# Flags by matmul, transposes at the beginning, loop hints on TensorE alone, last attention in a new order

## Chip, cores and metric

One core of a Trainium2 chip runs the whole program in one launch. The time is device microseconds of that core, as the median of several executions. One of them was also profiled; the profile's span runs from the first to the last instruction.

## The reference

The inputs are x (32 batches, 224 rows, 512), a context (32, 750, 384), a mask of rows, two gates and four weight matrices.

```python
def xattn(x, y, mask):                      # 16 heads of 32
    q = (x @ Wq.T), k, v = split(y @ Wkv.T)
    a = where(mask[:, None, :, None], q * 32**-0.5 @ k.T, -1e9)   # a masked row: all scores equal
    return softmax(a) @ v
def bitlinear(x, w, b):                     # rmsnorm, 8-bit rows, ternary weights
    return act_quant(rmsnorm(x)) @ weight_quant(w).T + b
x = x + tanh(g_xattn) * xattn(layernorm(x), ctx, mask)
x = x + tanh(g_ffn) * bitlinear(gelu(bitlinear(layernorm(x), w1, b1)), w2, b2)
```

weight_quant divides by the mean of |w| over the whole matrix, so no weight can be rounded before all have been read. A row outside the mask has equal scores, and its attention is the mean of v. With these inputs only the last quarter (56 rows) of a batch has rows that attend; the other three quarters use the mean.

## The kernel before, in words

All five engines have an instruction stream of their own, written out by hand, and meet by semaphores. The work has three parts.

**Beginning.** SyncE loads the context of batch 0 and the weights. ScalarE rounds them to the high part of a split of fp32 in two (`y_h`, `wkv_h`), VectorE takes the rest (`y_l`, `wkv_l`). VectorE reduces the mask bytes to `live_b` (a row for each batch), which SyncE brings through a DMA into one row, `live`; from that come `kind` (a number per batch) and `most` (their largest). Each engine's `Slow` loads `most` into a register, and `each` skips the code for batches that attend in more than the last quarter. There are none here, so all engines branch past it. GpSimd first increments some fifty semaphores by one (`primed`), and then fills the constants, the identity (`ident`) among them. TensorE waits for all six constants (`a_const`).

**Attention.** A period handles one batch b. It computes scores, softmax and weighted sum of b (four groups of four heads) interleaved with the k and v projections of batch b + 1, the loads of batch b + 2, and layer norm and quantising (the first half of the FFN) of batch b - 1: `summed` and `centred` and `rounded` on GpSimd, `x1_moments` and `x1_peak` on VectorE. One buffer set, f_x and f_c and so on, serves all batches; x1 and the rounded rows go to DRAM. Even and odd batches have different orders. In `batches`, every engine runs a period for batch -1 (projections alone), a loop of pairs up to batch 15, `middle`, a loop of pairs from batch 16 to 29, batch 30 written out, and `final` for batch 31. The loops carry a hint (`hint_back_edge`) for the branch at their end. Batches 0 to 15 also read a piece of w1 or w2 each, of which VectorE sums the magnitudes; in `middle` these sums become the mean (a matmul with `ones`), its inverse and three factors. Batches 16 to 31 read the pieces again, and GpSimd rounds them (`weights`).

**Last attention and FFN.** `final` interleaves batch 31's attention with the first steps of the FFN loop. There the 7168 rows go in 56 steps of 128: `inputs` (transpose), `widened` (first layer, 16 matmuls in two halves; VectorE adds b1 and scales), gelu and squares (ScalarE), root (GpSimd), `columns` (VectorE, its result is t_hs), `integers` (ScalarE), transposes, second layer, and the sum with x1 (GpSimd). TensorE works at transposes of step s - 2 and the second layer of step s - 3. The steps run as eight written out, a loop of eight (no hint), and the rest. The b1 row is loaded in `final`'s time and multiplied by a factor from the mean. Batch 31's layer norm is done in steps 2 to 7, in the same buffer set.

## Time and profile before

| | us |
|---|---|
| median of 3 executions | 1868.21 (1868.11 to 1868.63) |
| the profiled execution, its own time | 1867.66 |
| its span | 1865.9 |
| TensorE busy in the span | 1808.0 |
| VectorE, ScalarE, GpSimd busy | 1154.2, 990.6, 793.4 |

Times in the rows below are microseconds from the span's start. A row of the timeline has start, busy time, engine, line and operation, what it writes from what, shapes and count, and in brackets how long the engine was idle before and what released it. `issue` means that the profile shows nothing that it waited for.

### The profile page before, as it was taken

The numbers are of one execution on the slowest core, as the hardware profiler recorded it, in microseconds if no ns is written. First come the engines' busy times: TensorE is split into PE (matmuls) and PEld (weight loads), VectorE is DVE, ScalarE is ACT, GpSimd is POOL, SyncE is SP. The second block draws the span as 40 slices with busy tenths as digits, with TensorE's granted clock in tenths as the row PEclk, the third lists the DMA queues.
The fourth block names the chain that finished last, engine by engine and source line by source line (L and its number), as shares of the span: only waits on it lengthen the run. The fifth ranks groups of instructions, "written<-read, shape, count | busy, mean of one in ns | idle before, by whom it ended". The sixth has DMA issues, their size and how long they took to land.

```text
span 1865.9 us, 46309 instructions
## 1 busy us (share of the span) xinstructions
PE 1808.0 (97%) x16994; PEld 1395.2 (75%) x16995; DVE 1154.2 (62%) x2015; ACT 990.6 (53%) x1639; POOL 793.4 (43%) x1091
## 2 busy tenths in 40 slices
PE   5999999999999998999999999999977999999998
PEld 4888888888888887888888888888854555555554
DVE  2555556555555555555555555555558888888885
ACT  3444444444444443444444444444447888888886
POOL 1134344544433443556565555666544322222222
PEclk9999999999999999999999999999988999999999
DMA  4023322223223322222232232222133222222221
GB/s 146 14 79 108 91 88 73 78 73 93 73 80 113 90 81 74 79 73 78 74 92 73 82 119 85 78 73 73 61 103 100 78 85 84 76 79 84 82 91 44
DMA packets 83529, 153.91 MB, mean 82 GB/s; under 512 B 9725, under 2 KB 24061, under 8 KB 83341
## 3 DMA queue, kind: packets, MB, share of 16 engines
q1 hardware_dynamic: 83140, 152.89, 27.0%
q8 instruction: 33, 0.54, 0.1%
q10 hardware_dynamic: 328, 0.25, 0.1%
q14 instruction: 28, 0.22, 0.0%
HBM read 112.64 MB, written 40.46 MB: 82 GB/s over the span
## 4 chain that ended last, share of the span: by engine, by line
PE 89%; issue 3%; DVE 3%; ACT 2%; DMA 1%; POOL 1%; SPq 0%; POOLq 0%; DVEq 0%; ACTq 0%
PE psum L1383 23%; PE psum L1393 22%; PE psum L1403 9%; PE psum L1372 8%; PE psum L1618 8%; PE psum L1660 8%; PE psum L1412 5%; PE psum L1363 3%; PE psum L1646 2%; ACT hq L895 2%; DVE hid L1213 1%; PE psum L1420 1%; PE psum L1424 1%; DMA live<-live_b 1%; PE psum L1629 0%
## 5 line engine op out<-in xcount | busy, mean ns | idle before, releaser
L774 ACT ACTIVATE prob<-psum,nmax 114x750 f32<-114x750 f32 x256 | 225.5, 885 | 276.0 <-DVE nmax L1014 276.0
L1019 DVE TENSOR_TENSOR k_l<-psum,k_h 128x376 fp32r<-128x376 f32 (+1 forms) x256 | 139.7, 546 | 290.6 <-ACT k_h L765 290.6
L1383 PE MATMUL psum<-y_h,wkv_h 128*128 128x376 f32 (+1 forms) x768 | 277.2, 361 | 1.1 <-DVE q_l L1007 1.1
L1014 DVE TENSOR_REDUCE nmax<-psum 114x1 f32<-114x750 f32 x256 | 228.3, 933 | 76.2 <-PE psum L1372 73.4
L765 ACT ACTIVATE k_h<-psum 128x376 fp32r<-128x376 f32 (+1 forms) x256 | 124.0, 484 | 281.3 <-PE psum L1383 280.8
L1383 PE MATMUL psum<-y_l,wkv_h 128*128 128x376 f32 (+1 forms) x768 | 256.0, 333 | 0.0
L1383 PE MATMUL psum<-y_h,wkv_l 128*128 128x376 f32 (+1 forms) x768 | 255.7, 333 | 0.0
L1393 PE MATMUL psum<-wkv_h,y_h 128*125 128x512 f32 x576 | 239.0, 415 | 0.3 <-DVE wkv_l L1071 0.3
L340 POOL TENSOR_TENSOR f_x<-f_c,f_x 112x512 f32<-112x512 f32 x64 | 76.4, 1195 | 358.8 <-DMA f_c<-vmean_rows 338.1
L1393 PE MATMUL psum<-wkv_l,y_h 128*125 128x512 f32 x576 | 228.8, 397 | 0.0
L1393 PE MATMUL psum<-wkv_h,y_l 128*125 128x512 f32 x576 | 227.7, 395 | 0.0
L1618 PE MATMUL psum<-w_q,xq_t 128*128 128x512 bf16 x896 | 207.3, 385 | 4.1 <-DVE xq_t L1235 4.1
L1660 PE MATMUL psum<-w_q,hq_t 128*128 128x512 bf16 x896 | 202.6, 379 | 2.2 <-ACT yo L912 2.2
L1403 PEld LDWEIGHTS psum<-ident,prob 114*125 114x125 f32 x1536 | 186.0, 189 | 12.5 <-ACT prob L774 3.9
L1403 PE MATMUL psum<-ident,prob 114*125 114x114 f32 x1536 | 188.9, 273 | 5.5 <-ACT prob L774 5.5
L1028 DVE COPY prob_t<-psum 125x342 f32<-125x342 f32 x256 | 127.7, 510 | 96.5 <-PE psum L1403 85.7
L1618 PEld LDWEIGHTS psum<-w_q,xq_t 128*128 128x128 bf16 x896 | 84.6, 99 | 120.5 <-issue 21.5
L879 ACT ACTIVATE hid<-hid,gelu_in 128x1024 f32<-128x1024 f32 x112 | 127.8, 1143 | 82.3 <-DVE hid L1213 82.3
L607 POOL TENSOR_TENSOR y_l<-y,y_h 128x750 fp32r<-128x750 f32 x93 | 151.3, 1658 | 33.6 <-ACT y_h L760 33.6
L1660 PEld LDWEIGHTS psum<-w_q,hq_t 128*128 128x128 bf16 x896 | 85.2, 98 | 95.4 <-ACT yo L912 2.8
L1383 PEld LDWEIGHTS psum<-y_h,wkv_h 128*128 128x128 f32 x768 | 144.6, 188 | 14.7 <-DVE q_l L1007 1.5
L684 POOL TENSOR_SCALAR cols<-cols 128x1 f32<-128x1 f32 x56 | 10.8, 192 | 328.5 <-ACT hq L895 328.3
(120 smaller groups left out, 3372.2 us busy)
## 6 DMA issues: line engine op xcount, KB each, us to landing
y<-in_ctx_t SPq DMA_DIRECT2D x32, 1125.0 KB, 5.8
w_part<-in_w_t SPq DMA_DIRECT2D x32, 512.0 KB, 7.1
x_rows<-f_x SPq DMA_DIRECT2D x64, 224.4 KB, 2.8
x<-x_rows SPq DMA_DIRECT2D x56, 256.5 KB, 2.8
f_x<-in_x SPq DMA_DIRECT2D x64, 224.0 KB, 5.4
out_rows<-yo SPq DMA_DIRECT2D x56, 256.0 KB, 2.0
f_c<-vmean_rows SPq DMA_DIRECT2D x32, 224.0 KB, 6.2
xq_rows<-f_q SPq DMA_DIRECT2D x64, 112.0 KB, 2.7
```

The source lines that it names most:

```text
L607: pool.tensor_tensor(y_l[:, slot, c, :], y[:, c, :], y_h[:, slot, c, :].bitcast(F32), ALU.subtract).then_inc(f.yl, 1)
L774: act.activation(prob[:, e, :], ps_score[e][0:RP], ACT.Exp, bias=nmax[:, i:i + 1], accum_out=den[:, i:i + 1]).then_inc(p.exp, 1)
L879: act.activation(seg, seg, ACT.Gelu, scale=gelu_in[:, 0:1]).then_inc(t_g, 1)
L1014: dve.tensor_reduce(nmax[:, i:i + 1], ps_score[e][0:RP], AX.X, ALU.max, negate=True).then_inc(p.max, 1)
L1019: dve.tensor_tensor(k_l[:, g, s0:s1], ps_proj[k_bank[par][g, hf]][:, 0:s1 - s0], k_h[:, g, s0:s1].bitcast(F32), ALU.subtract).then_inc(f.k ...
L1028: dve.tensor_copy(prob_t[:, g % 2, e, MH:MJ, :].rearrange("p j n -> p (j n)"), ps_pt[e][1]).then_inc(p.pd, 1)
L1372: mm = pe.matmul(ps_score[e][0:RP, s0:s1], qs[r, slot, g, :, :].rearrange("p e r -> p (e r)"), ks[r, g, s0:s1], start=(n == 0), stop=(n == 2))
L1383: mm = pe.matmul(out_, ws[:, c, w], ys[:, slot, c, s0:s1], start=(c == 0 and n == 0), stop=(c == CC - 1 and n == 2))
L1393: mm = pe.matmul(out_, ys[:, slot, c, mcols], ws[:, c, D:], start=(c == 0 and n == 0), stop=(c == CC - 1 and n == 2))
L1403: mm = pe.transpose(ps_pt[e][hf][:, RP * j:RP * j + RP], prob[:, e, MC * jj:MC * jj + MC], ident[0:RP, 0:RP])
L1618: mm = pe.matmul(out_[:, BANK * o:BANK * o + BANK], xq_t[:, j % 2, 128 * c:128 * c + 128], w1_q[:, c, at_:at_ + BANK], start=(c == 0), sto ...
L1660: mm = pe.matmul(ps_y, hq_t[:, (j - LAG) % 2, 128 * c:128 * c + 128], w2_q[:, c, :], start=(c == 0), stop=(c == FC - 1))
```

## The change

- Flags: `live_rest` and `kind` are computed with a batch per partition in fp32 (`kind_b`), and turned into a row by a matmul with the identity into PSUM, which VectorE copies. The DMA goes. `ident` is filled before the `primed` increments, whose order changes. VectorE's and TensorE's `Slow` move ahead of other work.
- Beginning: TensorE issues 20 transposes of the identity, after three parts of y_h.
- Hints: only TensorE's two attention loops carry the hint; TensorE's batches 16 and 17 are written out (`peeled`).
- Mean: TensorE's matmul of `middle` moves behind the first scores of batch 16.
- Last attention: another order on VectorE and on TensorE, VectorE takes the two copies of the last group from ScalarE, GpSimd's `weights` goes first. SyncE issues the w2 piece ahead of the FFN's loads. Batch 30's layer norm is split between `final` and steps 2 to 7, batch 31's uses a second buffer set in v's slot 0 and goes on to step 48.

```diff
+        end_ = v[0:PT, 0].rearrange("p j n -> p (j n)")
...
+        sets.append((two(cut(2 * (D + 1))), two(cut(2 * D)), two(cut(D).bitcast(BF16)), two(cut(12)), two(cut(4)), two(cut(16))))
...
-        ENDS = (NT * 128 - S) // 128
+        ENDS = [(B - 2 + i) * S // 128 for i in range(2)]
...
-        primed = (a_w, a_wuse, a_wsum, a_wmm, a_wmean, c_st, *main.primed(), *aside.primed(), *last.primed(), *rest.primed())
+        primed = (*main.primed(), *last.primed(), a_w, a_wuse, a_wsum, a_wmm, a_wmean, c_st, *aside.primed(), *rest.primed())
...
-        def loop(eng, start, end):
-            return nc.Fori(start, end, engines=[eng.engine], hint_back_edge=True)
+        def loop(eng, start, end, hint):
+            return nc.Fori(start, end, engines=[eng.engine], hint_back_edge=hint)
...
-            with loop(eng, B // 4, B // 2 - 1) as t:
+            for b in range(B // 2, B // 2 + 2 * peeled):
+                period(b, b % 2, B // 4, True)
+            with loop(eng, B // 4 + peeled, B // 2 - 1, hint) as t:
...
     SyncE
-                sp.wait_ge(a_flag, 1)
-                sp.dma_start(live[:], live_b[:]).then_inc(a_live, 16)
...
+                    if w == 1:
+                        sp.wait_ge(f.x1, 2 * q)
...
                     if is_step(s, 2):
-                        ffn_load(B - 1, B - 1, False)
-                        copy_one(B - 2, c_end[0])
+                        stored(B - 1)
+                        ffn_load(B - 1, B - 1, False, main, 1)
                     if is_step(s, NT - RING):
-                        ffn_store(B - 1, B - 1)
+                        ffn_store(B - 2, B - 2)
+                    if is_step(s, ENDS[0] - 2):
+                        ffn_store(B - 1, B - 1, main, x1_d, xq_d, 1)
...
+                w2_piece(B - 1, B // 8 - 1, 1)
                 step(-1, -1, 0)
+                step(0, 0, 0)
+                step(1, 1, 0)
                 stored(B - 2)
                 ffn_load(B - 2, B - 2, False)
-                w2_piece(B - 1, B // 8 - 1, 1)
-                step(0, 0, 0)
-                ffn_store(B - 2, B - 2)
                 results(B - 1)
-                stored(B - 1)
-                run_steps(sp, step, 1, NT + LAG + 2)
+                run_steps(sp, step, 2, NT + LAG + 2)
...
     GpSimd
+                pool.memset(ident[:], 0.0).then_inc(own_ident, 1)
+                pool.wait_ge(own_ident, 1)
+                pool.affine_select(out=ident[:], in_=ident[:], compare_op=ALU.not_equal, fill=1.0, base=0,
+                                   pattern=[[-1, 128]], channel_multiplier=1).then_inc(a_const, 1)
+                pool.wait_ge(a_const, 1)
                 for s in primed:
                     pool.sem_inc(s, ONE)
...
                     for h in range(2):
-                        if is_step(s, 3):
-                            summed(B - 1, h)
-                        if is_step(s, 5):
-                            centred(B - 1, h)
+                        if is_step(s, 4):
+                            summed(B - 1, h, main, 1)
+                        if is_step(s, 6):
+                            centred(B - 1, h, main, 1)
+                        if is_step(s, NT - RING):
+                            rounded(B - 1, h, main, 1)
+                    for h in range(2):
+                        if is_step(s, 4):
+                            centred(B - 2, h)
                         if is_step(s, 7):
-                            rounded(B - 1, h)
+                            rounded(B - 2, h)
 
                 def final():
-                    for part in (summed, centred, rounded):
-                        for h in range(2):
-                            part(B - 2, h)
+                    weights(B - 1)
+                    for h in range(2):
+                        summed(B - 2, h)
                     step(1, 1, 0)
-                    weights(B - 1)
...
     ScalarE, final
-                    for e in range(2):
-                        first_half(last, n1, NG - 1, e)
...
     VectorE
-                dve.wait_ge(a_live, 16)
-                dve.tensor_reduce(live_rest[:], live[:, :, 0:NBLK - 1], AX.X, ALU.max).then_inc(a_flag, 1)
+                dve.wait_ge(a_flag, 1)
+                dve.tensor_reduce(live_rest[:], live_b[:, 0:NBLK - 1], AX.X, ALU.max).then_inc(a_flag, 1)
...
+                dve.wait_ge(a_live, 1)
+                dve.tensor_copy(kind[:], ps_kind).then_inc(a_flag, 1)
...
                     for h in range(2):
-                        if is_step(s, 4):
-                            x1_moments(B - 1, h)
+                        if is_step(s, 2 + h):
+                            x1_moments(B - 2, h)
+                        if is_step(s, 5):
+                            x1_moments(B - 1, h, main, 1)
                         if is_step(s, 6):
-                            x1_peak(B - 1, h)
+                            x1_peak(B - 2, h)
+                        if is_step(s, 7):
+                            x1_peak(B - 1, h, main, 1)
...
                     negated_max(last, n0, 0, 0)
                     negated_max(last, n0, 0, 1)
-                    dve.wait_ge(b_bias, 16)
-                    dve.tensor_scalar(b1_row[:], b1_row[:], bias_out[:], 1.0, ALU.mult, ALU.mult).then_inc(b_b1, 1)
                     second_half(last, n1, 0, 0)
                     second_half(last, n1, 0, 1)
                     inputs(0, 0)
                     negated_max(last, n0, 1, 0)
                     negated_max(last, n0, 1, 1)
+                    dve.wait_ge(b_bias, 16)
+                    dve.tensor_scalar(b1_row[:], b1_row[:], bias_out[:], 1.0, ALU.mult, ALU.mult).then_inc(b_b1, 1)
                     heads_out(last, b, 0)
-                    x1_moments(b - 1, 0)
-                    dve.wait_ge(b_b1, 1)
-                    widened(0, 0, 0, 0)
                     second_half(last, n1, 1, 0)
                     second_half(last, n1, 1, 1)
                     inputs(1, 1)
-                    x1_moments(b - 1, 1)
+                    dve.wait_ge(b_b1, 1)
+                    widened(0, 0, 0, 0)
...
+                    for e in range(2):
+                        second_half(last, n1, 3, e)
+                        dve.wait_ge(last.pt, n1 + (2 * (2 * 3 + e) + 1))
+                        dve.tensor_copy(prob_t[:, 1, e, 0:MH, :].rearrange("p j n -> p (j n)"), ps_pt[e][0]).then_inc(last.pa, 1)
                     widened(1, 1, 0, 0)
-                    second_half(last, n1, 3, 0)
-                    second_half(last, n1, 3, 1)
                     inputs(2, 2)
+                    heads_out(last, b, 3)
+                    peak(0, 0)
                     widened(1, 1, 0, 1)
-                    heads_out(last, b, 3)
                     divided(last, b, 32 * b + ONE)
-                    peak(0, 0)
...
     TensorE
-                pe.wait_ge(a_const, 6)
+                pe.wait_ge(a_const, 1)
+                pe.wait_ge(a_flag, 3)
+                pe.matmul(ps_kind, kind_b[:], ident[0:B, 0:B], start=True, stop=True).then_inc(a_live, 1)
+                pe.wait_ge(a_const, 7)
+                slow_pe = Slow(pe, "pe")
...
                     scores(last, 0, 0)
+                    if means:
+                        pe.wait_ge(a_wsum, 1 + ONE)
+                        pe.matmul(ps_w, ones[:], w_sum[:], start=True, stop=True).then_inc(a_wmm, 1)
...
+                    if means:
+                        pe.wait_ge(a_wmean, 1 + ONE)
                     weighted(last, n0, 0, 0)
...
                     inputs(2, 2, 0)
-                    widened(1, 1, 1)
                     pe.wait_ge(t_xe, 3)
                     weighted(last, n0, 1, 3)
+                    widened(1, 1, 1)
...
-                batches(pe, period, middle, final)
+                pe.wait_ge(a_yh, CC + ONE)
+                for i in range(20):
+                    pe.transpose(ps_warm, ident[:], ident[:])
+                batches(pe, period, lambda: None, final, 0, True, 1)
```

## Rows read from the trace of the kernel before

**Rows 1.** The page: span, chain that ended last by engine, a costly group.

```profile
span 1865.9 us, 46309 instructions
...
PE 89%; issue 3%; DVE 3%; ACT 2%; DMA 1%; POOL 1%; SPq 0%; POOLq 0%; DVEq 0%; ACTq 0%
...
L684 POOL TENSOR_SCALAR cols<-cols 128x1 f32<-128x1 f32 x56 | 10.8, 192 | 328.5 <-ACT hq L895 328.3
```

**Rows 2.** Chain that ended last, in order of time, 0 to 80: start, us, what.

```profile
6.14 9.70 DMA live<-live_b
...
22.75 4.17 PE psum L1393 x9
26.92 2.11 PE psum L1383 x9
29.03 2.11 PE psum L1393 x9
```

**Rows 3.** Timeline of GpSimd, 0 to 32.

```profile
6.61 0.10 POOL L592 MEMSET half<- 128x1 f32 x1 [6.15 <-issue]
```

**Rows 4.** Timeline of ScalarE, 0 to 32.

```profile
15.00 1.91 ACT L741 ACTIVATE wq_s<-w_q 128x2048 f32<-128x2048 f32 x1 [1.55 <-DMA w_q<-in_wq_t]
...
22.48 0.55 ACT L748 ACTIVATE xn_t<-psum 128x456 f32<-128x456 f32 x1 [5.48 <-PE psum L1356]
```

**Rows 5.** Timeline of TensorE, 0 to 60.

```profile
21.45 0.99 PE L1356 MATMUL psum<-ident,xa 114*128 114x114 f32 x4 [21.45 <-DVE xa L1000]
```

**Rows 6.** Timeline of TensorE: first scores of batches 14 to 18.

```profile
640.85 0.48 PE L1372 MATMUL psum<-k_h,q_h 64*114 64x512 f32 x2
...
680.75 0.48 PE L1372 MATMUL psum<-k_h,q_h 64*114 64x512 f32 x2
...
727.08 0.48 PE L1372 MATMUL psum<-k_h,q_h 64*114 64x512 f32 x2 [0.85 <-DVE w_cols L1197]
...
773.93 0.48 PE L1372 MATMUL psum<-k_h,q_h 64*114 64x512 f32 x2
...
817.72 0.49 PE L1372 MATMUL psum<-k_h,q_h 64*114 64x512 f32 x2
```

**Rows 7.** Timeline of VectorE, 718 to 738.

```profile
725.64 0.15 DVE L1189 TENSOR_REDUCE w_sum<-w_sums 128x2 f32<-128x16 f32 x1
...
727.07 0.20 DVE L1202 TENSOR_SCALAR y_out<-w_mean,gates 128x1 f32<-128x1 f32 x1
733.72 0.69 DVE L990 BATCH_NORM_STATS2 x_stats<-xa 114x6 f32<-114x512 f32 x1 [6.45 <-issue]
```

**Rows 8.** DMA queues, 720 to 740: queue, packets, MB, share.

```profile
q14 instruction: 3, 0.02, 0.3%
```

**Rows 9.** Timeline of TensorE, 1350 to 1425.

```profile
1370.65 0.97 PE L1372 MATMUL psum<-k_h,q_h 64*114 64x512 f32 x4 [5.59 <-DVE prob_t L1028]
...
1372.80 3.59 PE L1618 MATMUL psum<-w_q,xq_t 128*128 128x512 bf16 x8
...
1380.53 0.60 PE L1372 MATMUL psum<-k_h,q_h 64*114 64x512 f32 x4 [1.57 <-DVE prob_t L1028]
...
1381.75 1.90 PE L1618 MATMUL psum<-w_q,xq_t 128*128 128x512 bf16 x8
...
1405.97 1.89 PE L1646 MATMUL psum<-ident_h,hq 128*128 128x128 f16 x16 [5.33 <-ACT hq L886]
...
1419.37 3.62 PE L1660 MATMUL psum<-w_q,hq_t 128*128 128x512 bf16 x16
```

**Rows 10.** Timeline of VectorE, 1350 to 1425.

```profile
1368.37 1.28 DVE L1272 TENSOR_SCALAR b_row<-b_row,bias_out 128x2048 f32<-128x2048 f32 x1 [5.54 <-DMA b_row<-in_b]
1369.58 0.93 DVE L1028 COPY prob_t<-psum 125x342 f32<-125x342 f32 x2
...
1386.62 1.27 DVE L364 TENSOR_REDUCE f_cols<-f_c 112x1 f32<-112x512 f32 x2
...
1403.32 0.21 DVE L1227 TENSOR_SCALAR cols<-cols,y_out 128x1 f32<-128x1 f32 x1 [2.26 <-issue]
```

More of the change, by code:

```diff
@@ L271, in each, with batches @@
                     self.eng.sem_inc(met_slow, 1)
-        def loop(eng, start, end):
-            return nc.Fori(start, end, engines=[eng.engine], hint_back_edge=True)
-        def batches(eng, period, middle, final, first=0):
+        def loop(eng, start, end, hint):
+            return nc.Fori(start, end, engines=[eng.engine], hint_back_edge=hint)
+        def batches(eng, period, middle, final, first=0, hint=False, peeled=0):
             period(-1, 1, -1, False)
@@ L279, in batches @@
                 period(b, b, 0, False)
-            with loop(eng, first, B // 4) as t:
+            with loop(eng, first, B // 4, hint) as t:
                 for j in range(2):
@@ L1426, in sums, with even @@
                     mm.then_inc(p.rows, 1)
[L1428 removed]
+                def even(b, means):
                     n0, m = b * NP + ONE, b + 1
@@ L1593, in period @@
                     if j == 0:
-                        even(b)
+                        even(b, isinstance(b, int) and b == B // 2)
                     else:
                         odd(b, t, has_part(b), projects_ahead(b))
-                def middle():
-                    pe.wait_ge(a_wsum, 1 + ONE)
-                    pe.matmul(ps_w, ones[:], w_sum[:], start=True, stop=True).then_inc(a_wmm, 1)
-                    pe.wait_ge(a_wmean, 1 + ONE)
                 def low_halves(t, n):
```

90 lines of the change are left out of this document (49 added, 41 removed).

## The prediction

> **What bounds the kernel now.** The page comes first: span 1865.9 us, and the chain that ended last is TensorE for 89% [rows 1]. So what can be won is idle time of TensorE, and time in which it works at its lower clock (1.2 GHz and not 2.4). The second view to read is the start of each batch's first scores [rows 6]. From batch to batch they lie 39.90 us (even) and 43.79 us (odd) apart, without idle time inside. One pair stands out: 46.33 and 46.85 us where 43.79 and 39.90 are due, so the middle costs 2.54 + 6.95 = 9.5 us. The other two losses are at the ends of the attention: TensorE's first steady projection starts at 26.92 [rows 2], and between the last batch and the first second-layer matmul (1419.37 [rows 9]) stand idle times of 5.59 and 5.33 us [rows 9] and matmuls at half speed. The change touches all three places; I sum them against the profiled execution's own 1867.66 us, 1.8 us more than its span and 0.5 us under the median of 1868.21.
>
> **Start.** Before, VectorE sends the mask flags through a DMA; queued behind the big loads it lands 9.70 us later [rows 2], and everything VectorE does after it is late. The change replaces it by one small matmul on the identity, so GpSimd builds the identity before its 6.15 us of semaphore increments [rows 3] and not after them. VectorE's chain then follows its loads and is some 9 us earlier. What is late next? ScalarE, in whose order `turned` stands behind the wq copy: that waits for its load and runs 15.00 to 16.91 [rows 4]. Before, ScalarE turned only at 22.48; now it can from about 17.1, after the small `gates` and its branch past the unused code. The copy takes 0.55 us [rows 4], so the first k projection can start at 17.8, not 26.92: 9.1 us at best. Two things lie in between. The branch can need a code fetch; the two nearest prices are VectorE idles with no release in the profile, 2.26 us [rows 10] and 6.45 us under load [rows 7]. TensorE also issues 20 new transposes: four took 0.99 us at the low clock [rows 5], so 20 take at most 5.0 us; from the third y_h copy (about 9) they end at 14 if TensorE's own branch is through, at 17 if that is 3 us late, and then the 2.11 to 4.17 us of the first v chunk [rows 2] stand ahead of the k projection. I take a start at 19.2, nearer to the clean case since the copy hides most of the branch: 7.7 us. The lower bound is a k projection at 22.5 (fetch of 6.45 us from 16): 4.4 us. The transposes also raise the clock before the real work: nine v matmuls took 4.17 us and nine later ones 2.11 [rows 2]. The v part is now hidden in front of k; of k's 2.11 us, whose first half still ran at the low clock, I count 0.5 (0 to 1.0). Start: 8.2 us (4.4 to 9.6).
>
> **Middle.** The mean's tiny matmul now stands behind batch 16's first scores. That hides the 2.54 us wait: scores need nothing of the mean, and the sum is ready when they end. VectorE still runs its small instructions (from w_sum at 725.64 to y_out at 727.27, 1.6 us with their waits [rows 7]) ahead of the maxima of these scores, on which exp and the transposes wait. TensorE has two projections to do in between, so about 1.4 us of it shows. The other 6.95 us come from VectorE: it sat idle for 6.45 us with nothing that released it at its first instruction of the second loop [rows 7], TensorE then waited for exp and worked at the low clock around it. Three blocks of code were fetched in these 20 us [rows 8], while the same view over 200 to 460, loops running with hints, has none, nor has it over 1520 to 1760 (FFN loops, which carry no hint in either kernel). I read: the hint keeps the loop's head at hand and leaves the code behind the loop to be fetched after the exit. Without hints on VectorE the 6.95 go. Middle: 9.5 - 1.4 = 8.1 us (0 if the stall stays, 9.5 at most).
>
> A page speaks against this edit. The Trainium skill, Runtime: NRT & Kernel Launch, section Instruction fetch mechanics, says that prefetch is sequential and that a taken branch to a target outside the window of two pages has to be fetched first. By that an unhinted back edge could stall each time. The trace has the stall at the exit, not at the FFN loops' unhinted edges, so the rule's condition (a body too long for the window) decides; it is the fourth case below. TensorE keeps its hints and gets two batches outside the loop; they are the same instructions without the branch, and I cost that at nothing.
>
> **Last attention and ramp.** (a) VectorE idled 5.54 us for the b1 row [rows 10] ahead of the copies that free the score banks, and TensorE 5.59 us with it [rows 9]. Now two copies, `inputs` and two maxima (3 to 4 us of work) come first, by when the row has landed. The release for TensorE's second scores moves from behind the scaling's end (1369.65) and two copies to where VectorE's idle of 5.54 us began, less what the transposes take: near 1365.4 in place of 1370.65, 5.2 us. (b) They and the next eight matmuls ran at the low clock: 1370.65 to 1372.80 and 3.59 us, later 1380.53 to 1381.75 and 1.90 us [rows 9]. Without the pause: 0.9 + 1.7 = 2.6 us. (c) VectorE sheds two statistics with a small instruction each (the like of them took 0.69 us [rows 7]) and two peaks (1.27 together [rows 10]), some 2.9 us, and takes over two half copies from ScalarE, 0.9 us: 2.0 net; half of it is on the path, 1.0. (d) GpSimd's rounding of the w2 piece moves before the first FFN row's root, and TensorE's last weighted sum ahead of the last hidden matmul: 0.9 us, within the bound 0 to 2. (e) The 2.26 us idle without a releaser in `columns` [rows 10] is of the fetch kind and sets t_hs, ScalarE's integers and TensorE's 5.33 us idle. It goes with the hint or comes back elsewhere; I take 2.0. Against it: the w2 piece is now issued ahead of xq and x1 of step 1, so the second `inputs` waits about 0.6 us. Sum 5.2 + 2.6 + 1.0 + 0.9 + 2.0 - 0.6 = 11.1. The other ramp idles stay. Bounds: 7 (c to e nothing, b half) to 15 (all, and the 5.33 us idle short enough that the clock stays up).
>
> **What is moved into the FFN.** Batch 30's layer norm now runs in steps 2 to 7, batch 31's up to step 48, in a second buffer set lying in the v slot that the last attention doesn't read. GpSimd idles 328.5/56 = 5.9 us per step ahead of its root [rows 1]. Step 4 gets two sums and two centrings, about 8 us, so 2 us over: that delays one root by 2 us, against VectorE's and ScalarE's idle time before it. Cost 0, at worst 2 us once. VectorE gets at most 1.7 us more in a step. The loads and stores (SyncE) are issued some steps ahead of the rows that need them: nothing. The price if that cover is gone is one late store, 3 us.
>
> **Sum.** 8.2 + 8.1 + 11.1 = 27.4. 1867.7 - 27.4 = 1840.3; with the 0.5 us to the median, 1840.8 us.
>
> **Rivals.**
> 1. The forecast: 1841, own range 1834 to 1848. Chance 0.62.
> 2. The exit stall is no matter of hints: any first entry to new code costs VectorE a fetch, at 727 under a 1.1 MB load. For it: straight code in `columns` stalled too. Against: in the whole list of waits these two are VectorE's only idles without a releaser, and its first loop's first entry has none. The 6.95 us stay, and with the delayed mean the middle gives 1 us: 1848. Chance 0.17.
> 3. A new wait in the last attention: xq and x1 behind the w2 piece, or ScalarE's table load and gelu setting the pace, and low clock through the ramp as before. The end gives 5 us in place of 11.1: 1847. Chance 0.13.
> 4. The other side: unhinted back edges stall. VectorE's two attention loops have six back edges each, at the even batch's start, where the middle showed what an idle of 6.45 us costs TensorE: 6.95 us. 12 x 6.95 = 83 us, 1841 + 83 = 1924. For it: VectorE's attention body is longer than its FFN body of eight steps, and it is the only one with this length. Against: the FFN body is nearly as long and fetches nothing. It decides from 27.4/12 = 2.3 us per edge on, about the smaller of the two idle times. Chance 0.06.
> 5. Small cover losses at all places: 1855 to 1866. Chance 0.02.
>
> **Range and chances.** Cases 1 to 3 lie between 1834 and 1855; with case 4 and what lies beyond left out, 1834 to 1853 holds about 8 in 10. A difference of 0.2% (3.7 us) is about what a measurement can tell from none. Faster: cases 1, 2, 3 and most of 5, 0.92. Same 0.02, slower 0.06.
>
> **What would show it.** After: no DMA of `live`; first steady k projection near 19 us; first scores of batches 15 to 17 about 43.8 and 39.9 us apart, 1.4 more in all, with no idle of VectorE over 2 us; b1's scaling without idle ahead of it; second-layer matmuls of step 0 some 27 us earlier than 1419.37; FFN steps as long as before. Wrong if code fetches appear every 84 us on VectorE with idle behind them, if ScalarE's first turn comes later than 21, or if GpSimd's step 4 makes TensorE idle.

## The result and the profile after

The kernel after takes 1852.89 us (median, 1851.26 to 1853.91), the kernel before on the same chip 1868.36: ratio 0.9919 [0.9904, 0.9934]. The forecast was 1841, with 1834 to 1848 as its own range and 1834 to 1853 for about 8 in 10. The sign was right, but the gain was 15.5 us where 27.4 were forecast; that the time lies 0.1 us inside the wider range confirms nothing. The profiled execution after took 1853.91 us with a span of 1852.2, so 13.7 of span were gained against the 1865.9 of [rows 1].

Read the timeline of TensorE in the order of the chain. The first group is the beginning, beside [rows 2] and [rows 5]:

```profile
15.41 4.50 PE L1808 MATMUL psum<-ident 128*128 128x128 f32 x20 [10.12 <-issue]
19.70 0.97 PE L1390 MATMUL psum<-ident,xa 114*128 114x114 f32 x4
20.35 0.73 PE L1427 MATMUL psum<-wkv_h,y_h 128*125 128x512 f32 x1
...
22.76 0.34 PE L1417 MATMUL psum<-y_h,wkv_h 128*128 128x376 f32 x1
...
50.49 0.60 PE L1406 MATMUL psum<-k_h,q_h 64*114 64x512 f32 x4
```

TensorE stood idle until 15.41 with nothing in the profile that it waited for (`issue`), then ran the 20 transposes, and only then turned xa. ScalarE, which the prediction took for the limit, waited for it:

```profile
17.44 0.19 ACT L771 ACTIVATE gates<-gates_in 128x2 f32<-128x2 f32 x1
20.71 0.55 ACT L776 ACTIVATE xn_t<-psum 128x456 f32<-128x456 f32 x1 [3.08 <-PE psum L1390]
```

The first k projection starts at 22.76 (before 26.92, forecast 19.2), the first scores at 50.49, where they were at 55.05: 4.6 us. The middle, beside [rows 6] (first scores of batches 15 to 17):

```profile
676.21 0.60 PE L1406 MATMUL psum<-k_h,q_h 64*114 64x512 f32 x4
...
719.99 0.60 PE L1406 MATMUL psum<-k_h,q_h 64*114 64x512 f32 x4
...
725.90 0.91 PE L1437 MATMUL psum<-ident,prob 114*125 114x114 f32 x6 [0.48 <-ACT prob L802]
...
761.66 0.60 PE L1406 MATMUL psum<-k_h,q_h 64*114 64x512 f32 x4
```

The distances are 43.78 and 41.67 us, where they were 46.33 and 46.85. And VectorE's first instruction of the second loop comes without the 6.45 us of [rows 7]:

```profile
722.52 0.21 DVE L1231 TENSOR_SCALAR y_out<-w_mean,gates 128x1 f32<-128x1 f32 x1
722.96 0.69 DVE L1019 BATCH_NORM_STATS2 x_stats<-xa 114x6 f32<-114x512 f32 x1 [0.24 <-DVE y_out L1231]
```

All steady distances are as before (39.91 and 43.78 us), but one is new: batch 30, right behind the exit of TensorE's second loop, takes 43.36 us where 39.91 are due. TensorE stops inside its first scores with no releaser in the profile, and then works at the low clock for some 3 us (0.63 us for a matmul that takes 0.39):

```profile
1307.56 0.49 PE L1406 MATMUL psum<-k_h,q_h 64*114 64x512 f32 x2
1309.65 0.37 PE L1406 MATMUL psum<-k_h,q_h 64*114 64x238 f32 x2 [1.60 <-issue]
...
1311.26 0.63 PE L1427 MATMUL psum<-wkv_h,y_l 128*125 128x512 f32 x1
...
1314.25 0.48 PE L1417 MATMUL psum<-y_h,wkv_h 128*128 128x376 f32 x1
...
1350.92 0.60 PE L1406 MATMUL psum<-k_h,q_h 64*114 64x512 f32 x4
```

The last attention and the ramp, beside [rows 9]. From batch 31's first scores to the first second-layer matmul it is 1350.92 to 1401.52, 50.60 us, where it was 59.63:

```profile
1357.05 0.97 PE L1406 MATMUL psum<-k_h,q_h 64*114 64x512 f32 x4 [0.27 <-DVE prob_t L1057]
...
1359.11 1.90 PE L1652 MATMUL psum<-w_q,xq_t 128*128 128x512 bf16 x8
...
1378.32 0.81 PE L1446 MATMUL psum<-prob_t,v 125*32 125x57 f32 x48 [2.40 <-DVE xq_t L1264]
1379.06 3.29 PE L1652 MATMUL psum<-w_q,xq_t 128*128 128x512 bf16 x8
...
1387.67 1.07 PE L1680 MATMUL psum<-ident_h,hq 128*128 128x128 f16 x16 [1.10 <-ACT hq L914]
...
1394.10 6.47 PE L1652 MATMUL psum<-w_q,xq_t 128*128 128x512 bf16 x16 [5.14 <-DVE xq_t L1264]
```

The FFN, where the prediction had nothing to lose, loses 2.2 us: from the first to the eleventh second-layer matmul it is 82.51 us, before 80.29. The timeline of GpSimd in step 4 (from 1409.16 sums and centrings without a gap, then the root at 1417.33, with no idle time before it):

```profile
1409.16 2.34 POOL L356 TENSOR_TENSOR v<-v 112x512 f32<-112x512 f32 x2
...
1416.16 1.09 POOL L377 TENSOR_TENSOR f_x<-b_row,f_x 112x512 f32<-112x512 f32 x1
1417.33 0.19 POOL L708 TENSOR_SCALAR cols<-cols 128x1 f32<-128x1 f32 x1
```

VectorE's columns wait for that root, ScalarE's gelu waits for what VectorE adds behind them, and the distance of ScalarE's squares, about 8.1 to 8.3 us elsewhere, is 10.00 there:

```profile
1418.19 0.21 DVE L1252 TENSOR_SCALAR cols<-cols 128x1 f32<-128x1 f32 x1 [1.88 <-POOL cols L710]
```

```profile
1413.23 1.89 ACT L923 ACTIVATE hq<-hid 128x2048 bf16<-128x2048 f32 x1
...
1420.19 1.15 ACT L907 ACTIVATE hid<-hid,gelu_in 128x1024 f32<-128x1024 f32 x1 [2.70 <-DVE hid L1242]
...
1423.23 1.89 ACT L923 ACTIVATE hq<-hid 128x2048 bf16<-128x2048 f32 x1
```

At the very end one second-layer group takes 5.32 us; the same sixteen matmuls take 3.63 at the high clock, as they did in the profiled execution of before: 1.7 us.

```profile
1833.29 5.32 PE L1694 MATMUL psum<-w_q,hq_t 128*128 128x512 bf16 x16 [1.40 <-ACT yo L940]
1838.44 1.06 PE L1680 MATMUL psum<-ident_h,hq 128*128 128x128 f16 x16
1839.39 3.63 PE L1694 MATMUL psum<-w_q,hq_t 128*128 128x512 bf16 x16
```

| part | forecast | measured |
|---|---|---|
| start (first scores of batch 0) | 8.2 | 4.6 |
| middle (first scores 15 to 17) | 8.1 | 7.7 |
| batch 30 | 0 | -3.45 |
| last attention to first second layer | 11.1 | 9.0 |
| FFN ramp and loop | 0 | -2.2 - 0.2 |
| clock at the end | 0 | -1.7 |
| sum | 27.4 | 13.75 |

### The profile page after: what moved, and what is told of

Same layout as the page of the kernel before. It is cut to its first block, busy times and chain, and to the rows that moved or that the text cites. A ratio compares the mean times of both kernels' runs of the same rounds, so it can differ in the third digit from the quotient of the medians.

```text
span 1852.2 us, 46262 instructions
## 1 busy us (share of the span) xinstructions
PE 1811.3 (98%) x17016; PEld 1395.8 (75%) x17017; DVE 1153.6 (62%) x2018; ACT 989.3 (53%) x1637; POOL 791.9 (43%) x1091
## 4 chain that ended last, share of the span: by engine, by line
PE 89%; issue 4%; DVE 3%; ACT 3%; POOL 1%; DMA 0%; POOLq 0%; DVEq 0%; ACTq 0%
PE psum L1417 23%; PE psum L1427 22%; PE psum L1437 9%; PE psum L1406 8%; PE psum L1652 7%; PE psum L1694 7%; PE psum L1446 5%; PE psum L1397 3%; ACT hq L923 2%; PE psum L1680 2%; DVE hid L1242 1%; PE psum L1454 1%; PE psum L1458 1%; POOL cols L710 0%; PE psum L1390 0%
## 5 line engine op out<-in xcount | busy, mean ns | idle before, releaser
L708 POOL TENSOR_SCALAR cols<-cols 128x1 f32<-128x1 f32 x56 | 10.7, 190 | 331.1 <-ACT hq L923 331.0
```

## The experiments

Each of the sixteen kernels is the kernel after with the edit shown, if nothing else is said. A ratio is to the kernel before on the same chip, whose medians were 1865.79 to 1867.33 us there, against 1868.36 beside the kernel after. So a difference of under some 3 us between two medians tells nothing. For single microseconds the distances inside the traces are used, one profiled execution each; the start (first scores at 49.6 to 50.5 in nine executions with the same beginning) and the end (below) scatter in these too.

### The hints

Hints back on all engines (`hint=True` as the default in `batches`, so on the loops of VectorE, ScalarE and GpSimd together):

> The kernel after, with the hint on the attention loops of all engines again, as before the change. Theory A (the hint is what made VectorE idle for 6.45 us at its first instruction of the second loop): the idle time returns in the middle, at x_stats, and the distance of the first scores of batches 16 and 17 goes from 41.67 to about 48 us: 6 to 7 us more, 1859.5. Theory B (any first entry to new code costs it; in the kernel after it only fell well): the distance stays at 41.7 and the time at 1852.9. Steady distances (39.91 and 43.78 us) stay in both.

Measured: 1860.26 us, 0.9963 [0.9949, 0.9977]; batch 16 takes 49.39 us and not 41.67. VectorE's timeline has both idles without a releaser again, that of the middle and, 1.7 us of loss in the ramp (52.30 us for 50.60), that of `columns`:

```profile
728.38 0.69 DVE L1019 BATCH_NORM_STATS2 x_stats<-xa 114x6 f32<-114x512 f32 x1 [6.33 <-issue]
...
1399.05 0.21 DVE L1252 TENSOR_SCALAR cols<-cols 128x1 f32<-128x1 f32 x1 [2.79 <-issue]
```

The other direction, the kernel before with this one part of the change, again for these three engines together:

> The kernel before with one part of the change alone: the hint on TensorE's two loops only, none on the other engines' attention loops. Theory A (the hint on VectorE made its idle of 6.45 us at the second loop's first instruction): that idle goes, first scores of batches 16 and 17 stand 39.9 to 41.5 us apart and not 46.85, batches 15 and 16 still 46.3; the last attention also gains the 1.7 us that the reverse test lost: 1860 in all. Theory B (the gain in the middle came from where the mean's matmul stands and from the two batches written out, the hint only decides together with them): under 2 us of gain, 1866 or more.

Measured: 1857.63 us, 0.9958 [0.9944, 0.9972]. Batch 15 still 46.33, batch 16 now 41.40; x_stats starts 0.24 us after the instruction ahead of it:

```profile
726.92 0.69 DVE L990 BATCH_NORM_STATS2 x_stats<-xa 114x6 f32<-114x512 f32 x1 [0.24 <-DVE y_out L1202]
```

The last attention takes 55.19 us where it took 59.63: 4.4 us more gained, from the hints alone. In spans, this one edit gives 10.2 us, where the whole change gives 13.7. Theory A, larger than expected. That VectorE's hint is the one that counts among the three is read from its idle times and was not tried by itself.

No hint at all, TensorE's last argument pair `True, 1` made `False, 1`:

> The kernel after, without the hint on TensorE's two loops either, so that no loop of the kernel carries it. Theory A (for TensorE the hint keeps the pass running at the loop's end; without it the head of the loop is fetched after the branch): an idle of 1 to 4 us at each of TensorE's back edges, twelve or thirteen in all, first scores of even batches late by that: 1865 to 1900. Theory B (as on VectorE, a back edge without a hint costs nothing, and the exit gets better): distances of 43.78 and 39.91 us in all pairs, batch 30 too: 1849.5.

Measured: 1896.72 us, 1.0149 [1.0117, 1.0181]. Most batches of both loops take 1.4 to 2.8 us more, with 2.2 us idle at a back edge. The view of the DMA queues says why: q8, which brings TensorE's code in blocks of 16 KB, has no entry from 200 to 600 after, and here

```profile
q8 instruction: 42, 0.69, 0.7%
```

So an unhinted back edge does cost on TensorE (2.17 us of `issue` at 224.66, for one), while the kernel after has no idle time of that kind on VectorE.

### Where TensorE's code lies

The same edit in several sizes, in `slow_first`, which no engine executes here:

```diff
                     pe.wait_ge(a_wqs, 1)
+                    for _ in range(64):          # 192 and 128 in the next two
+                        pe.wait_ge(a_wqs, 1)
```

> The kernel after, with 64 more wait instructions for TensorE in the code for batches that attend in more than the last quarter. No engine executes that code with these inputs; it only moves all TensorE code behind it by 64 instructions. Theory A (the 43.36 us between the first scores of batches 30 and 31, where 39.91 is due, come from where TensorE's second loop ends against the blocks in which its code is fetched): the distance is 39.9 again, no idle of TensorE without a releaser stands behind the loop's exit, and the time is 3.4 us lower than the kernel after, near 1849.5. Theory B (leaving a hinted loop costs TensorE a fetch wherever its code lies, or the stall belongs to the two batches written out): the distance stays at 43.4 and the time at 1852.9. In both, the branch at the start may cost more or less than before, by up to 3 us, which is read from TensorE's first transposes.

Measured: 1882.96 us, 1.0084 [1.0067, 1.0101]. Batch 30 takes 39.91 us, as theory A has it, but batches 19 to 28 take up to 46.3 us, 28.8 more in all, and batch 16 takes 4.2 more. The DMA view of 900 to 1300 (none of these rows in the kernel after):

```profile
q8 instruction: 40, 0.66, 0.7%
```

40 blocks in 400 us are nine for each pass of some 89 us, while a pass has 1843 instructions in the trace, 7.2 blocks.

> The kernel after, with 192 more wait instructions for TensorE in the code that no engine executes, where the run before this one had 64. TensorE's code is fetched in blocks of 16 KB, 256 instructions of 64 bytes, so 192 more is the same place in the blocks as 64 fewer. One pass of an attention loop has some 1843 instructions on TensorE in the trace's records, 7.2 blocks. Theory A (a loop whose body touches eight blocks stays, one that touches nine is fetched anew in each pass, and code just behind a block's border at the exit is late): the second loop ends some 80 instructions ahead of a border, so neither occurs: batches 19 to 29 at 43.78 and 39.91 us, batch 30 at 39.91, and 3.4 us less than the kernel after, 1849.5. Theory B (every shift away from the code's old place has such a cost, by something other than blocks): losses in several batches as in the run with 64.

Measured: 1894.68 us, 1.0142 [1.0122, 1.0162]. Now the second loop and batch 30 are clean (43.78, 39.91), and the first loop is fetched anew: batches 1 to 14 take 43.3 to 46.4 us. The same view, 200 to 600:

```profile
q8 instruction: 41, 0.67, 0.7%
```

> The kernel after, with 128 more wait instructions for TensorE that no engine executes. Theory A (what decides is where a loop lies against the blocks of 256 instructions; the second loop lies 57 further in a block than the first, by the number of instructions in the trace; a shift of 64 costs the second loop, 192 the first, so the costly part reaches at least from 121 to 192 behind the first loop's old place): with 128 the first loop is at 128 and the second at 185, both inside, so both are fetched anew in each pass: batches 1 to 14 and 19 to 29 each 1 to 5 us longer, about 70 us in all, 1915 to 1930. Theory B (the place of each loop decides in no such simple way): only one loop or none is slower, under 1900.

Measured: 1851.60 us, 0.9921 [0.9904, 0.9937]. Neither loop is fetched anew, so theory A of this run fell. In its place the first loop's exit stalls (batch 15 at 45.88 us) and the second's doesn't (39.91):

```profile
721.82 0.60 PE L1406 MATMUL psum<-k_h,q_h 64*114 64x512 f32 x4 [2.03 <-issue]
```

I read: a loop of 7.2 blocks touches eight, or nine when its end lies a little behind a border. Eight stay, nine are fetched anew in each pass; an end just ahead of a border gives the stall at the exit. This picture is argued and not shown, since no trace has the addresses. For the second loop the stall is at shift 0 and the fetching at 64; for the first at 128 and at 192. That the two lie 128 apart, and not the 57 that I had counted, was fitted afterwards. And one thing it doesn't explain: with a shift by a whole block (three kernels below) batch 30 also takes 39.91 us. By the Trainium skill (Runtime: NRT & Kernel Launch, Instruction fetch mechanics) TensorE's instruction memory holds 2048 instructions and is filled in blocks of 256, which is eight blocks. The 0.66 MB in 40 packets agree with the block's size, and that nine blocks in a pass are fetched anew agrees with its eight. The window of two pages, which the prediction quotes from the same section of the Trainium skill, does not agree with TensorE's hinted loops here: passes of 7.2 blocks run from 200 to 600 with no entry on q8, and the measurement decides.

The stall at the exit is not the same in all kernels that have it. With the same TensorE code, the kernel of `The FFN's step` below (centring in step 3) idles a little less, its clock stays high, and batch 30 takes 41.60 us and not 43.36:

```profile
1309.45 0.37 PE L1406 MATMUL psum<-k_h,q_h 64*114 64x238 f32 x2 [1.43 <-issue]
```

So of the 3.45 us about half is the stall and half the low clock behind it.

### The start

Without the 20 transposes (their two lines deleted, 40 unexecuted instructions in their place):

> The kernel after, without the 20 transposes of the identity at the beginning; 40 instructions that no engine executes keep the code behind them in its place. Theory A (the transposes stand on the path, and the clock that they raise gives back less than they take): TensorE turns xa at 15.4 to 15.5, the first v chunk takes 4.0 to 4.2 us at the low clock, and the first scores of batch 0 start near 48.5 us where they start at 50.49 with the transposes; the time is 2 us lower. Theory B (the prediction's: they fit into waiting time and give a warm start): first scores at 50.5 or later, up to 51.2.

Measured: 1847.96 us, 0.9897 [0.9881, 0.9914]; first scores at 48.40. The transposes cost 2.1 us here; over all kernels, first scores stand at 49.6 to 50.5 in the nine with them behind the branch and at 47.1 to 48.4 in the five without any. The rest of this time's gain is not the start's: batch 30 takes 41.43 us, with an idle time of 1.45 and no low clock. Moved ahead of the branch instead:

```diff
+                for i in range(20):
+                    pe.transpose(ps_warm, ident[:], ident[:])
                 pe.wait_ge(a_const, 7)
                 slow_pe = Slow(pe, "pe")
```

> The kernel after, with the 20 transposes of the identity right behind the flags' matmul, ahead of the branch past the unused code and not behind it (and written to another bank). Theory A (the branch costs TensorE until about 15.4 whatever it does before, since a fetch stands behind it, and the transposes behind it then cost 4.5 us of the start): TensorE turns xa at about 15.5 where it did at 19.7, ScalarE's copy is ready at 17.4 to 18, the first k projection starts between 18 and 21 where it started at 22.93, and the time is 2 to 4 us lower, about 1850. The first v chunk may run at the low clock then, 4.2 in place of 2.25 us. Theory B (ScalarE, with the wq copy and the gates, is the limit of the start, or the fetch only begins when TensorE reaches the branch and is late by as much as the transposes take): the first k projection stays within 1 us of 22.9.

Measured: 1852.98 us, 0.9918 [0.9902, 0.9935], and yet first scores at 48.47; this profiled execution lost 1.2 us more than after at the end's clock. TensorE turns xa at 15.53, whether transposes were done before or not, and the clock has fallen again by then (0.63 us a matmul):

```profile
5.40 4.53 PE L1384 MATMUL psum<-ident 128*128 128x128 f32 x20
15.53 0.99 PE L1392 MATMUL psum<-ident,xa 114*128 114x114 f32 x4 [5.60 <-issue]
16.20 0.77 PE L1429 MATMUL psum<-wkv_h,y_h 128*125 128x512 f32 x1
16.77 0.63 PE L1429 MATMUL psum<-wkv_l,y_h 128*125 128x512 f32 x1
```

With 60 of them, to fill that idle time, and with the centring in step 3 (next section) and 176 unexecuted instructions:

> The kernel after with 60 transposes of the identity right behind the flags' matmul, ahead of the branch (another bank), in place of 20 behind it, and GpSimd's first centring of batch 30 in step 3; 176 instructions that no engine executes make the shift of TensorE's code a whole block. Theory A (TensorE's stream reads on while its matmuls run, so the fetch behind the branch overlaps the transposes, and they fill the idle time until 15.5 with work): the turn of xa still starts near 15.5, the first v chunk runs at the high clock (2.2 us and not 4.2), first scores at 46.5 to 47.5, time 1844 to 1845. Theory B (the fetch begins only when the transposes are through, near 14): the turn starts at 17 to 20 and the first scores stand at 48.5 to 50.5: 1847 to 1849.

Measured: 1850.25 us, 0.9907 [0.9893, 0.992]. Theory B: first scores at 50.26. The idle time moves with them, 4.09 us behind their end, and the clock is low all the same. The fetch moves too: the first block of TensorE's code behind the branch starts on q8 at 12.7 in the kernel after and in the two above, and at 14.7 here, and each time the first matmul follows its landing by 1.6 to 1.8 us.

```profile
4.88 8.79 PE L1384 MATMUL psum<-ident 128*128 128x128 f32 x60
17.77 0.99 PE L1392 MATMUL psum<-ident,xa 114*128 114x114 f32 x4 [4.09 <-issue]
```

### The FFN's step

GpSimd's first centring one step earlier:

```diff
                     for h in range(2):
-                        if is_step(s, 4):
+                        if is_step(s, 3 + h):
                             centred(B - 2, h)
```

> The kernel after, with GpSimd's first centring of batch 30 in FFN step 3 and not in step 4; the second stays. GpSimd's block in step 4 goes from 8.1 to some 5.4 us. Theory A (the FFN's step is set by a ring of squares, root, columns, second half of the first layer, gelu, squares, so that every delay of GpSimd's root is paid in full): root is not late in step 4, the distance of the squares there falls from 10.00 to about 8.6 us, and all later squares and the end come 1.4 us earlier, 1851.5. Theory B (the prediction's: TensorE has work to do meanwhile, and the delay is absorbed): the squares of steps 10 and later stand where they stood against the first squares, and the time is 1852.9.

Measured: 1849.47 us, 0.9905 [0.9889, 0.9922]. The squares of this stretch, 8.26 and 8.08 us apart:

```profile
1401.84 1.89 ACT L923 ACTIVATE hq<-hid 128x2048 bf16<-128x2048 f32 x1
1410.10 1.90 ACT L923 ACTIVATE hq<-hid 128x2048 bf16<-128x2048 f32 x1
1418.18 1.90 ACT L923 ACTIVATE hq<-hid 128x2048 bf16<-128x2048 f32 x1
```

First to eleventh second layer: 80.63 us for 82.51, 1.9 us kept to the end. This profiled execution is 6.4 us faster than that of the kernel after; the rest is batch 30 (1.8), the last attention (1.35) and the clock at the end (1.65), which the edit was not made for. The sharper test of what sets the step, one small instruction more in GpSimd's root:

```diff
+                        pool.tensor_scalar(c[:, HMS:HMS + 1], c[:, HMS:HMS + 1], 1.0, 0.0, ALU.mult, ALU.add).then_inc(own_ms, 1)
+                        pool.wait_ge(own_ms, 2)
                         pool.tensor_tensor(c[:, HR:HR + 1], c[:, HMS:HMS + 1], half[:], ALU.pow).then_inc(t_hr, 1)
```

> The kernel after, with one more small instruction of GpSimd (a multiplication by one) between the two of the FFN's root, in each of the 56 steps: some 0.28 us more in GpSimd's root, at an engine that idles for about 6 us in each step. Theory A (the ring of squares, root, columns, second half, gelu, squares sets the step of 8.14 us): the step becomes 8.4 us and the time 13 to 15 us more, about 1867. Theory B (the prediction's premise, TensorE sets the step and the other engines' idle time is cover): the step stays within 0.02 us of 8.14, and the time at 1852.9.

Measured: 1868.14 us, 1.0007 [0.9997, 1.0016]. 15.2 us more, from 0.27 us on an engine that is idle for some 6.1 in each step:

```profile
1602.32 0.19 POOL L708 TENSOR_SCALAR cols<-cols 128x1 f32<-128x1 f32 x1 [6.26 <-ACT hq L925]
1602.59 0.19 POOL L710 TENSOR_SCALAR cols<-cols 128x1 f32<-128x1 f32 x1
...
1610.73 0.19 POOL L708 TENSOR_SCALAR cols<-cols 128x1 f32<-128x1 f32 x1 [6.09 <-ACT hq L925]
```

The step is 1610.73 - 1602.32 = 8.41 us, where it was 8.14, and TensorE, without idle time there in the kernel after, now has some in each step:

```profile
1607.13 3.62 PE L1654 MATMUL psum<-w_q,xq_t 128*128 128x512 bf16 x16 [0.21 <-DVE xq_t L1266]
```

### The b1 row

VectorE's two lines with `bias_out` moved back ahead of `second_half(last, n1, 0, 0)`:

> The kernel after, with VectorE's scaling of the b1 row put back ahead of the copies of the first group, where it stood before the change. Theory A (the prediction's term: the wait for the row is worth 5.2 us, and the clock behind it up to 2.6 more): VectorE idles 3 to 6 us ahead of the scaling, TensorE's second scores start some 11 us after the first ones and not 6.1 us, and the first second-layer matmul stands 5 to 8 us later after batch 31's first scores: 1858 to 1861. Theory B (the row lands early enough now, or later waits, as ScalarE's, absorb the delay): under 2 us, 1853 to 1855.

Measured: 1858.80 us, 0.9956 [0.9939, 0.9972]. VectorE waits 5.36 us for the row again, and TensorE's second scores start 10.7 us after the first (in the kernel after, 6.1):

```profile
1361.31 0.97 PE L1406 MATMUL psum<-k_h,q_h 64*114 64x512 f32 x4 [4.51 <-DVE prob_t L1057]
```

But from batch 31's first scores to the first second layer it is 54.27 us for 50.60, so only 3.7 us reach the FFN. At the fourth group's weighted sum the difference is still 5.3 us: 1383.33 - 1350.59 = 32.74 here, 1378.32 - 1350.92 = 27.40 in the kernel after. The next eight matmuls and the last sixteen of the first layer are at the high clock for longer here, 1.90 us for 3.29 and 5.66 for 6.47:

```profile
1383.33 0.81 PE L1446 MATMUL psum<-prob_t,v 125*32 125x57 f32 x48 [2.40 <-DVE xq_t L1264]
1384.07 1.90 PE L1652 MATMUL psum<-w_q,xq_t 128*128 128x512 bf16 x8
...
1398.24 5.66 PE L1652 MATMUL psum<-w_q,xq_t 128*128 128x512 bf16 x16 [5.15 <-DVE xq_t L1264]
```

### The best version

Centring in step 3 and no transposes:

> The kernel after with two of the single changes together: without the 20 transposes (40 instructions that no engine executes in their place), and with GpSimd's first centring of batch 30 in FFN step 3. Theory A (the two gains are at different places of one chain and add): first scores near 48.4 us, 80.6 us from the first second-layer matmul to the eleventh, and 3.5 to 4.5 us less than the kernel after: 1846. Theory B (the second is taken back by VectorE's and ScalarE's own delays in steps 3 to 5): no more than 2 us less, 1848 or more.

Measured: 1844.24 us, 0.9875 [0.986, 0.989]. First scores at 47.06, first to eleventh second layer 80.58 us: both gains are there, the start's larger than by the single edit. Batch 30 takes 41.43. With 226 unexecuted instructions more:

> The run with both single changes together, with 226 more instructions that no engine executes, which is 30 fewer against the blocks of 256. Theory A (the stall behind the exit of TensorE's second loop goes when the code behind it lies a few instructions further from the border, and both loops still stay in the buffer): batch 30 at 39.91 us, all others as before, 1.5 to 3.5 us less than with both: 1843. Theory B (the first loop's head comes into the part of a block where the loop is fetched anew, as with 192): batches 1 to 14 each 2 to 5 us longer, 1890 or more.

Measured: 1889.85 us, 1.0112 [1.0092, 1.0133]: theory B, the first loop (40 blocks from 200 to 600). With a whole block more:

> The run with both single changes (no transposes, centring in step 3), with 256 more instructions that no engine executes. Theory A (the run with 60 transposes had batch 30 at 39.91 us because its code lay a whole block further, which pairs of blocks or the buffer's slots notice): batch 30 at 39.91 us, first scores of batch 0 near 47.1 to 48.4, 1.5 us less than without: 1842.7. Theory B (a whole block changes nothing; the clean exit there was another timing of the fetch): batch 30 at 41.4 us, 1844.2.

Measured: 1843.35 us, 0.9879 [0.9862, 0.9895], batch 30 at 39.91 in the profiled execution. The median is 0.9 us lower than without the block (the two kernels' executions overlap), so the gain itself is not shown. And with matmuls in the two idle times at the end (twelve of w1 against the identity in step 56, seven ahead of `pe.wait_ge(t_hq, k + 1)` behind a wait for t_he, five ahead of the wait for t_ye):

> The run with both single changes and the whole block's shift, with twelve extra matmuls of TensorE in FFN step 56, whose results nobody reads: seven ahead of the transposes that wait 1.75 us for ScalarE, five ahead of the second layer that waits 1.40 us. Theory A (these idle times let the clock fall in some executions, and the 16 matmuls behind them then take 6.55 us and not 3.63): the matmuls take 3.63 us, and the end stands 25.0 us after the fourth last second layer's start in all executions; times spread over less than 2 us, median 1 to 2 us below the same without them, about 1841. Theory B (the filling matmuls themselves delay the last steps, or the clock falls by another cause): the same time or up to 1 us more.

Measured: 1843.41 us, 0.9879 [0.9862, 0.9895], spread 1842.53 to 1844.10, against 1842.36 to 1844.87 without. The added matmuls cost nothing, and whether they hold the clock is not told: in both profiled executions the group behind them took 3.63 us. These last two are the best versions, 22.6 us under before on their chip, where the kernel after is 15.5 under before on its own.

## Where the prediction failed and where it held

Of the 13.65 us between the forecast's 27.4 and the table's 13.75, two terms that the prediction put at nothing make 5.9: batch 30 (3.45) and the FFN (2.4). Two that it mis-sized make 5.7: the start (3.6) and the last attention (2.1). The clock at the end (1.7), which it doesn't have, and the middle (0.4) are the rest.

**Start (8.2, measured 4.6).** The DMA wait and VectorE's delay went as said. The step that failed is the pricing of the 20 transposes and of the branch ahead of them: I let the transposes start at about 9, or 3 us later, and ScalarE's copy be the limit. TensorE, with the branch past the unused code in this stretch, stood idle until 15.41, 10.12 us after the flags' matmul; my worst case was 6.45 us of fetch from 16 on, a k projection at 22.5, and 22.76 lies just outside it. The transposes stood whole on the path behind it: 2.1 us net, since they spare 9 v matmuls the low clock but take 4.5. That the branch waits for a block of code is read from q8, whose block lands at 13.8 and moves with the transposes, and from the idle's `issue`; it was not isolated.

**Middle (8.1, measured 7.7).** The sum is right, and both reasons act. The wait of 2.54 us went, and 1.76 remained visible in batch 16 where 1.4 were forecast. But the shares are not the forecast's 6.95 for the hint and 1.1 for the mean, and that the sum fits is in part luck. Batches 15 and 16 together take 93.18 us before and 93.17 with all hints in the new order: as long as the hints are there, moving the mean and writing out two batches is worth nothing. Without the hints they are worth 2.3 (87.73 to 85.45), and the hints' going is worth 5.45 in the kernel before and 7.7 in the kernel after. Rival 2 is ruled out: the stall comes with the hints and goes with them, in both kernels.

**Batch 30 (0, measured -3.45).** "They are the same instructions without the branch, and I cost that at nothing" is the sentence that failed. Two batches written out, and the transposes, move TensorE's second loop against the blocks of its code. The shifts show that the place matters: the same executed instructions lose 3.45 us at this exit and nothing in the loops, or 29 to 46 us in one of the loops, or 2.1 us at the other exit. At one place the loss still varies (43.36 and 41.60), with the low clock behind the stall. Rival 4 was false for VectorE and true for TensorE. That it is the number of blocks that a pass touches is the picture above, and stays argued.

**Last attention (11.1, measured 9.0).** Terms (a) and (b), together 7.8, were mis-sized: undone, they return 3.7. The b1 wait was 4.6 and not 5.2; the second scores still ran at the low clock (0.97 us); and of the 5.3 us that are there at the fourth group, the low stretches at 1379.06 and 1394.10, longer than with the wait, take part back. This stretch takes 49.0 to 51.9 us in kernels where nothing of it was changed, so single differences of 1 to 2 us are no more than that scatter; the three kernels nearest in batch 30 (43.36 to 43.40) have 50.5 to 50.6. Terms (c) to (e), together 3.3, were 9.0 - 3.7 = 5.3, by subtraction. Of these the fetch in `columns`, forecast at 2.0, returned 1.7 when undone; in the old order the hint alone was worth 4.4. How the rest divides among (c) and (d) was not tried. Rival 3 was half true: the 2.40 and 5.14 us waits for xq_t with low clock behind them are what it named.

**FFN (0, measured -2.4).** The premise failed, not the size: GpSimd's idle time ahead of its root is no cover. The root's delay goes on through VectorE's columns, its second half of the first layer, ScalarE's gelu and squares back to the root, a ring that sets the step of 8.14 us: 0.27 us more in it gave 8.41. TensorE's own work fits in 8.02 (1409.55 to 1417.57, from one second layer to the next). Why the steps written out at the end take 8.08 and not 8.14 is open. I had foreseen the 2 us of delay in step 4 and took it as "against VectorE's and ScalarE's idle time"; both idles are parts of the ring's waiting for the others. Its worst case, 2 us once, is what was paid: 1.9 of it came back with the centring in step 3.

**End (0, measured -1.7).** The same two idle times (1.75 and 1.40 us) stand there before and after. The group behind them takes 5.0 to 6.6 us in nine of the ten profiled kernels in which GpSimd does both centrings of batch 30 in step 4, and 3.63 in the tenth (all hints) and in all eight others, before among them. So it may well go with the change, by when the FFN comes to its end; why is open, and the test with matmuls in these idle times stood on a kernel that has no low clock there without them.

## What to carry over

Ask of an idle engine whether it stands in a ring that sets the step: then its idle time is other engines' work, and a delay that it adds is paid, once or in each step (0.27 us in each of 56 steps gave 15.2 us). An edit that only adds or removes instructions of a long loop's engine moves the loop against its code blocks; look at the queue that brings code, and try two or three shifts with instructions that are never executed before judging the edit. A hint for a loop's back edge should be tried engine by engine: here it costs some 6 us of idle time at the exit of VectorE's short loop and saves some 40 us on TensorE's long ones.

## What the runs showed of the hardware that I had not expected

- Code placement alone is worth up to 43 us of 1853 here (1851.60 to 1894.68 us, four places of the same executed instructions).
- A loop that is refetched takes nine blocks a pass (40 in 400 us) and shows as `issue` idles of up to 2.5 us, with matmuls at the low clock behind them in each pass (0.63 for 0.39 us).
- Work ahead of a taken branch doesn't hide all of the idle time behind it: TensorE's first matmul behind it started at 15.4 to 15.7 us with 0 or 20 transposes before it, at 17.8 with 60, each time at the low clock.
- Two idle times of 1.75 (2.02 in one kernel) and 1.40 us, with 1.07 us of transposes between them, stand ahead of the same 16 matmuls in seventeen of the eighteen profiled kernels, and the clock fell behind them in nine: 5.0 to 6.6 us where the others take 3.63.
